# Where the even blocks' turned tiles lie in a partition: 960 bytes left free ahead of them

## The reference, cut to what matters

```python
xn = layernorm(x)                        # x: 2 x 4096 tokens, 512 wide
# branch 1: a state-space scan over the tokens, then a GELU layer
x1 = xn + ssm_scan(rmsnorm(xn, scale1), A, B, C, D)      # 16 states for each channel
h  = rmsnorm(x1, scale2)
h  = gelu(h @ w1 + b1) @ w2 + b2         # w1: 512 x 2048, w2: 2048 x 512
# branch 2: a gated layer on inputs and weights rounded to FP4 in groups of 16
g  = fp4(xn) @ fp4(w_gate).T;  u = fp4(xn) @ fp4(w_up).T # 1408 wide
z  = fp4(silu(g) * u) @ fp4(w_down).T
out = x + (x1 + h) + z
```

## Time and profile before

| what | us |
|---|---|
| median of the three runs | 3148.84 (3148.7 to 3151.13) |
| the profiled execution's own time | 3149.97 |
| its span, first to last instruction | 3148.1 |
| DVE busy | 2048.0 (65%) |
| ACT busy | 1086.4 (35%) |
| POOL busy | 1148.1 (36%) |

### The profile page before, as it was taken

The page is one execution under the profiler, slowest core; times in us unless marked ns, Lnnn a source line. Parts: engine busy times, 40 slices in busy tenths (PEclk is TensorE's granted clock), DMA queues, the critical chain, the costliest instruction groups (busy, mean ns, idle before and its releaser), DMA issues.

```text
span 3148.1 us, 43122 instructions
## 1 busy us (share of the span) xinstructions
PE 3064.3 (97%) x14861; PEld 2471.4 (79%) x14861; DVE 2048.0 (65%) x4427; ACT 1086.4 (35%) x1910; POOL 1148.1 (36%) x1097
## 2 busy tenths in 40 slices
PE   5899999999999999999999999999999999999999
PEld 3678788888877777777777788888888888888887
DVE  8798898987777776767777754444445444444442
ACT  5445655644543433434323321111212211221211
POOL 7556656655555555555554210110101111111000
PEclk9999999999999999999999999999999999999999
DMA  4133333357766666566633533333333333333320
GB/s 124 44 90 89 116 114 119 94 137 184 183 175 172 162 155 179 156 161 166 171 87 94 131 73 73 73 68 74 77 64 81 74 71 71 71 72 72 71 60 14
DMA packets 865577, 335.58 MB, mean 107 GB/s; under 512 B 680400, under 2 KB 771792, under 8 KB 862800
## 3 DMA queue, kind: packets, MB, share of 16 engines
q1 hardware_dynamic: 865360, 332.83, 43.1%
HBM read 225.21 MB, written 107.51 MB: 106 GB/s over the span
## 4 chain that ended last, share of the span: by engine, by line
PE 69%; DVE 16%; issue 5%; POOL 5%; ACT 2%; DMA 2%; SPq 1%; DVEq 0%; POOLq 0%; ACTq 0%
PE bank L894 22%; PE bank L878 22%; PE bank L755 13%; PE bank L777 7%; DVE qs L998 3%; POOL qa L1544 2%; DVE qa L1015 2%; PE bank L818 2%; DVE qs L1009 2%; DVE qa L971 2%; DVE qb L1023 1%; POOL qa L1538 1%; PE bank L826 1%; PE bank L725 1%; DVE sg L963 1%
## 5 line engine op out<-in xcount | busy, mean ns | idle before, releaser
L878 PE MATMUL bank<-hT,Wp 128*128 128x512 f32 x3072 | 743.5, 391 | 2.5 <-DVE Wp L1185 2.0
L894 PE MATMUL bank<-Wp,G 128*128 128x512 f32 x3072 | 743.9, 391 | 0.0
L878 PEld LDWEIGHTS bank<-hT,Wp 128*128 128x128 f32 x3072 | 576.5, 188 | 128.0 <-issue 2.4
L894 PEld LDWEIGHTS bank<-Wp,G 128*128 128x128 f32 x3072 | 576.7, 188 | 126.2
L755 PE MATMUL bank<-XT,Wu 128*128 128x512 f32 (+1 forms) x2148 | 515.6, 389 | 16.9 <-DVE sg L963 16.7
L755 PE MATMUL bank<-XT,Wg 128*128 128x512 f32 (+1 forms) x2148 | 524.6, 393 | 6.4 <-DVE Wd L1030 6.4
L777 PE MATMUL bank<-Wd,HT 128*128 128x512 f32 x2112 | 516.1, 393 | 7.4 <-POOL HT L1552 6.0
L1234 DVE CAST G<-gf 128x512 fp32r<-128x512 f32 x256 | 110.8, 433 | 607.9 <-PE bank L894 588.7
L755 PEld LDWEIGHTS bank<-XT,Wu 128*128 128x128 f32 x2148 | 400.8, 190 | 107.7 <-issue 26.9
L777 PEld LDWEIGHTS bank<-Wd,HT 128*128 128x128 f32 x2112 | 391.8, 188 | 107.4 <-issue 15.4
L755 PEld LDWEIGHTS bank<-XT,Wg 128*128 128x128 f32 x2148 | 398.8, 190 | 95.5 <-DVE Wd L1030 8.5
(11 more groups left out here) (114 smaller groups left out, 2826.4 us busy)
## 6 DMA issues: line engine op xcount, KB each, us to landing
px<-in_L_attn_x_dram SPq DMA_DIRECT2D x128, 256.0 KB, 3.4
xin<-in_L_attn_x_dram SPq DMA_DIRECT2D x128, 256.0 KB, 3.5
sT<-r_K SPq DMA_DIRECT2D x128, 256.0 KB, 4.2
r_Z<-xin SPq DMA_DIRECT2D x64, 256.0 KB, 2.3
r_U<-ub SPq DMA_DIRECT2D x16, 1024.0 KB, 6.6
sU<-r_U SPq DMA_DIRECT2D x32, 512.0 KB, 5.0
r_Y<-sY SPq DMA_DIRECT2D x16, 1024.0 KB, 5.4
xl<-in_L_attn_x_dram SPq DMA_DIRECT2D x64, 256.0 KB, 3.0
```

Source lines behind the costliest of these rows:

```text
L878: ins = e.matmul(bk[:], Wp[f][wh][:, 0, k * P:(k + 1) * P], hT[xh][b % 2][:, k, :], start=(k == 0 and p_ == 0), stop=(k == KD - 1 and p_ = ...
L894: ins = e.matmul(ACC[j][:], G2[gh][:, n % 2, j * P:(j + 1) * P], Wp[f][wh][:, 1, :], start=(f == 0 and p_ == 0), stop=(f == 15 and p_ == 2))
```

## The change

```diff
@@ build
         sg = sbt(actx, "sg", [P, 512])
         st6 = sbt(actx, "st6", [P, 2, 6])
+
+        sbt(actx, "pad6", [P, 240])
 
         pctx = ExitStack()
         px = sbt(pctx, "px", [P, 4, D])
```

## The result

The changed kernel takes 3137.58 us, the median of five runs (3135.42 to 3138.68), against 3149.28 before, now also the median of five (3148.70 to 3151.13); the ratio is 0.996 with a 95% interval of 0.9949 to 0.9971. That is 11.7 us less. The forecast was 3137.5 us, 11.3 less than the 3148.84 known then.

The account below looks back on a forecast made before the run. PE, busy 97% of the span, was taken to bound the kernel, in the last stage by time per matmul group. 10.4 us (blocks 2 to 14) plus 0.84 (block 0) gave 11.3 off 3148.84: 3137.5 us, range 3134.0 to 3143.0.

Parts of the forecast that it names:

- The rate of the even blocks: Last stage, blocks 2 to 14: seven even blocks go from 88.53 to 87.04 us, 1.49 us each, 10.4 us.
- The step named as the cause: GELU products: `hT0` lies 960 bytes off the weights, no multiple of 512; the change makes the distance one, giving odd-block rate.
- the prediction's argument from L894: L894 never reads `hT0` yet costs 2.77 us beside it; a slow region would let it recover within its first matmuls.
- Block 0: Last stage's first block: 9 steps after PE's waits gain 0.093 us each, 0.84 us; ends 0.8 and 1.5.
- the second wait: Block 0 at 1773.31 us: PE waits for ACT's `gf`; the gain was counted from here to 1823.21.
- the first wait: Block 0 until 1767.07 us: PE waits 2.02 us for DVE's `Wp`; what PE gains before, it waits longer.
- The bound that took all 16 steps as gaining: Block 0: upper end of its gain, 1.5 us if every step gains, against 0.84 forecast.
- the first zero: Middle stage: the scan's operands move together, so costed at nothing; bound 2.3 us either way, 1.8% of 127 us.
- the second zero: Transfers into moved tiles such as `yl0`: costed at nothing, sizes, pieces and order being the same; bound 2.6 us either way.
- The absolute place: Rival: reads of `hT0` are slow because it lies highest in the partition, not by distance; no change, 3148.8 us; chance 0.10.
- The writes: Rival: ACT and DVE writing `hT1` slow PE; odd blocks 1 to 13 turn slow, 10.4 us more, 3159.3 us; chance 0.04.
- part of the slowness: Rival, last stage: a rest of the slow rate may remain; half the gain would give 3143.2 us; chance 0.06.

Follow-up runs that it names:

- all but `hT0`: Against the kernel before: `zx0`, `xl0`, `yl0`, `zl`, `b2r` moved to 1,376 modulo 2,048, `hT0` left at 416; 3147.05 us in one run.

## Why the prediction was right, point by point

**The rate of the even blocks.** 7 x 1.49 = 10.4 us were expected of blocks 2 to 14; from the start of block 1 to the end the trace is 10.4 us shorter. The step named as the cause, the distance of `hT0` from the weights, is shown from both sides: `hT0` alone brings the gain, the other tiles alone nothing, a common shift changes nothing, and moving the weights of the other product by 64 bytes slows that product in all blocks. Of the prediction's argument from L894 the single matmuls leave this: L894 does come back to its pace, but at 416 it needs ten of its twelve matmuls for it.

**Block 0.** 0.84 us were expected from the second wait on and 0.8 came. (A step of 5.533 us is 88.53 / 16; nine are 49.80 and not the 49.90 of the row, since the first group after the wait takes 0.1 us longer, in both kernels. The gain isn't touched by it.) Before the first wait PE kept nothing of its gain, as the step said: counted from the start of the last stage it came to the wait 0.3 us earlier (31.80 and 31.50 us) and waited 2.56 us for 2.02. How much longer it waits can't be read from one pair, as this wait runs from 1.3 to 3.5 us over the profiles. The bound that took all 16 steps as gaining was not needed.

**The zeros.** The scan's operands were put at nothing with a bound of 2.3 us, the transfers into moved tiles with one of 2.6. The kernel that moves the middle stage's tiles alone is at 0.9998 [0.9988, 1.0008], which is 3.8 us faster to 2.5 us slower, so the first zero stands within the measurement. The two windows with the scan take 20.31 us after, as they took 20.30 before:

```profile
1148.75 2.88 PE L757 MATMUL bank<-XT,Wg 128*128 128x512 f32 x12
...
1169.06 2.20 PE L757 MATMUL bank<-XT,Wg 128*128 128x512 f32 x9
```

`yl0`, on which the second zero rests, is among the tiles of "all but `hT0`": from its start to its end the last stage takes 3145.3 - 1730.95 = 1414.4 us there and 3148.1 - 1733.25 = 1414.9 in the kernel before. Ahead of that stage no effect can be told apart: the three profiles with `yl0` at 416 begin it between 1730.14 and 1733.25 us, the five with `yl0` at 1,376 between 1730.62 and 1732.91. The DVE, ACT and POOL busy times of blocks 2 and 3 agree within 0.5 us before and after.

**The 1.1 us too many.** The profile pair shows 12.3 us and not 11.3. The rest lies ahead of the second wait in block 0. The prediction's sign that the span before 1733 us would stay within 1 us did not come: the last stage began 1.35 us earlier, and block 1 1.9 us earlier in place of 1. The other profiles show differences of up to 3.5 us in that start, with and without moved tiles, so the change need not have made this one; what makes it vary is not shown. The medians' difference, 11.7 us, is nearer to the sum.

**The rivals.** The absolute place fell with `hT0` 17 KB higher and fast, with all tiles 64 bytes higher and the same, and with `hT0` slow 64 and 128 bytes higher but fast at 192. The writes fell in the changed kernel itself: ACT and DVE write `hT0` at 1,376 in its odd blocks, which still take 87.04 us. No part of the slowness remained. The Trainium skill's sentence that "PE and ACT never wait on anyone" (SBUF — State Buffer, "Who interferes with whom") would have had all these kernels within the noise of one another; between the distances of 768 and 928 bytes block 2 differs by 2.13 us of 87.04 with the same instructions, so for TensorE's own two operands the measurement goes against it.

**What the step had too narrow.** The forecast said a multiple of 512 bytes, read off from the weight blocks' step and from `HT` at 352. The condition is weaker: 256 bytes do, in the moving operand's place (768) and in the weights' (256). The number forecast did not depend on it, but a smaller gap would have done: 192 bytes for 960.

**What stays open.** Why it is 256 bytes is not shown. That the weight load of one matmul and the moving stream of the one before it disturb each other is an inference from both of them counting; no run here took the two apart in time. That L894, with its operands in step, pays as much as L878 at 416 and less at 480 comes from its ten late matmuls for three; why the recovery takes so many is not shown. It isn't bound to `hT0`'s place: in the changed kernel too, behind the 1.06 us that PE is idle before 1735.85, about eleven matmuls come late before the pace of 0.227 us is back. Tried in the last stage were distances from 0 to 960 bytes, with this type and 512 columns alone.

## What to carry to other kernels

When PE is busy all the time and groups of the same shape come at two distances, look at what changes at the edge, and at the tiles' addresses. In a kernel of this kind lay the stationary and the moving tile a multiple of 256 bytes apart; small tiles in between shift all that follows. Here `qs` with its 1,024 bytes does no harm, as L777's operands, 1,024 apart, are fast; it is the 48 bytes of `st6`, which take up 64, that leave the rest off a multiple of 256. A pad costs nothing but its bytes, and 192 were enough here for 0.4% (3137.58 us, in one run).

## What the runs showed of the hardware that was not expected

Matmuls of 512 columns in this type come every 2.72 / 12 = 0.2267 us where the operands' distance is a multiple of 256 bytes. Off it, L878's group costs up to 1909.86 - 1907.05 = 2.81 us, with `hT0` at 448 (timeline, block 2's first two groups):

```profile
1907.05 2.98 PE L878 MATMUL bank<-hT,Wp 128*128 128x512 f32 x12
1909.86 2.92 PE L894 MATMUL bank<-Wp,G 128*128 128x512 f32 x12
```

The worst of the distances tried was the one that is no multiple of 64, and a tile's start is rounded to 32 bytes only; so a small tile laid ahead of an operand cost up to 89.17 / 87.04 = 2.4% of the blocks that read it. And the price is not kept to the product with the distance: its neighbour in the stream, with nothing wrong of its own, pays 0.02 to 0.05 us a group, until three to ten of its matmuls have passed.
